# Window attention and shifted blur: queries and keys stacked by way of DRAM, the residual read back in four quarters

## The reference, cut to what matters

```
x = x + L0(_gn(x), w_qkv, w_proj, b_proj, bias_table, rel_index)
x = x + L1(_gn(x), offset)

L0: qkv = einsum('bchw,oc->bohw', x, w_qkv)     # cut into 7x7 windows, 12 heads of 16
    dots = einsum('wnid,wnjd->wnij', q, k) * scale + bias
    out = einsum('wnij,wnjd->wnid', softmax(dots), v)
    return einsum('bchw,oc->bohw', out, w_proj) + b_proj
L1: each of 8 groups of 24 channels is displaced by its own offset, rounded,
    and then filtered with a 5x5 Gaussian that is centred on the offset's rest
```

## Time and profile before

| | before |
|---|---|
| median of 3 runs | 5955.9 us (5952.99 to 5961.64) |
| the profiled execution's own time | 5947.59 us |
| its span in the trace | 5945.8 us |
| PE busy | 5372.8 us, 90% |
| PEld, DVE, ACT, POOL busy | 75%, 72%, 64%, 60% |
| mean granted TensorE clock | 0.936 of full |
| mean rate of the DMA engines | 133 GB/s |

### The profile page before, as it was taken

One profiled execution on the slowest core, in us unless ns is written; L12 is line 12 of the kernel. 1 busy time (PEld: TensorE's weight loads), 2 busy tenths in 40 slices (PEclk: granted clock), 3 DMA queues, 4 the chain that ended last, 5 costly groups with the idle time before them and its releaser, 6 DMA issues.

```text
span 5945.8 us, 259453 instructions
## 1 busy us (share of the span) xinstructions
PE 5372.8 (90%) x98232; PEld 4462.4 (75%) x98232; DVE 4278.6 (72%) x9682; ACT 3798.7 (64%) x8451; POOL 3556.2 (60%) x3940
## 2 busy tenths in 40 slices
PE   4998999999999999999999999999999999999996
PEld 3777777777777777777777777777777777777775
DVE  3777777777777777777777777777777777777773
ACT  1666666666666666667666666666666666666662
POOL 0566556666566666566665566665666655566664
PEclk9999999999999999999999999999999999999996
DMA  2566665666665666655666655666656666656653
GB/s 60 128 139 143 141 139 129 135 138 143 138 138 124 143 136 144 142 133 126 143 137 141 142 132 130 141 139 136 145 125 134 138 141 139 139 128 136 137 129 65
DMA packets 1353356, 790.32 MB, mean 133 GB/s; under 512 B 1187912, under 2 KB 1237512, under 8 KB 1344392
## 3 DMA queue, kind: packets, MB, share of 16 engines
q1 hardware_dynamic: 1352200, 774.03, 58.6%
HBM read 157.09 MB, written 154.14 MB: 52 GB/s over the span
## 4 chain that ended last, share of the span: by engine, by line
PE 37%; SPq 33%; issue 10%; ACT 8%; DVE 6%; DMA 5%; POOL 0%; ACTq 0%; DVEq 0%; POOLq 0%
SPq L414 13%; SPq L420 11%; PE pO L641 6%; SPq L432 5%; PE pT L624 3%; DMA xr<-x_scratch 2%; PE pS L598 2%; PE pS L590 2%; PE pM L509 2%; PE pT L617 2%; PE pT L608 2%; PE pM L511 2%; PE pM L510 1%; PE pO L651 1%; DMA kst<-mix 1%
## 5 line engine op out<-in xcount | busy, mean ns | idle before, releaser
L1222 POOL TENSOR_TENSOR probl<-prob,probh 98x588 f16<-98x588 f32 x1024 | 1332.2, 1301 | 398.3 <-DVE probh L1066 287.8
L1228 POOL TENSOR_TENSOR o<-osb,o 128x192 f16<-128x192 f32 x1024 | 598.6, 585 | 1434.0 <-ACT o L860 1414.9
L641 PEld LDWEIGHTS pO<-vv,probh 98*49 98x49 f16 x24576 | 866.2, 121 | 206.7 <-issue 151.6
L641 PE MATMUL pO<-vv,probh 98*49 98x34 f16 x24576 | 1017.7, 225 | 1.4 <-ACT om L868 1.2
L641 PE MATMUL pO<-vv,probl 98*49 98x34 f16 x12288 | 990.0, 228 | 2.3 <-issue 2.3
L852 ACT ACTIVATE mov<-pT 12x98 f16<-12x98 f32 x1024 | 244.6, 239 | 993.9 <-PE pT L608 992.7
L1051 DVE TENSOR_REDUCE mx<-pS 128x12 f32<-128x588 f32 x1024 | 776.7, 759 | 18.9 <-PE pS L598 6.1
L641 PEld LDWEIGHTS pO<-vv,probl 98*49 98x49 f16 x12288 | 765.9, 121 | 2.4 <-issue 2.4
L847 ACT ACTIVATE prob<-pT 98x588 f32<-98x588 f32 x1024 | 671.7, 656 | 147.0 <-PE pT L624 133.0
L624 PE MATMUL pT<-qst,kst 96*98 96x49 f16 x12288 | 750.8, 207 | 1.0 <-issue 0.8
L590 PE MATMUL pS<-biasT,addb 128*64 128x294 f16 x4096 | 617.5, 310 | 124.9 <-DMA kst<-mix 77.7
(11 more groups left out here) (192 smaller groups left out, 16086.5 us busy)
## 6 DMA issues: line engine op xcount, KB each, us to landing
kst<-kh SPq DMA_DIRECT2D x1536, 98.0 KB, 2.2
qst<-qh SPq DMA_DIRECT2D x1536, 49.0 KB, 2.4
qst<-mix SPq DMA_DIRECT2D x768, 98.0 KB, 2.6
kst<-mix SPq DMA_DIRECT2D x768, 98.0 KB, 2.5
vv<-cv SPq DMA_DIRECT2D x1024, 73.5 KB
xr<-x_scratch SPq DMA_DIRECT2D x64, 1176.0 KB
out<-xr SPq DMA_DIRECT2D x256, 294.0 KB
x_scratch<-xm SPq DMA_DIRECT2D x256, 196.0 KB, 3.2
```

What stands on the lines that cost most here:

```text
L641: mm = pe.matmul(pO[64 * win:64 * win + NT, OW * hp:OW * hp + OW], b[0:98, p % 2, PW * hp + NT * win:PW * hp + NT * win + NT], vv[:, g % 2 ...
L1222: pool.tensor_tensor(probl[0:98, p % 2, :], prob[0:98, p % 2, :], probh[0:98, p % 2, :], ALU.subtract).then_inc(S["pl_p"], 1)
L1228: pool.tensor_tensor(o16[:, p % 2, C:2 * C], osb[:, p % 2, :], o16[:, p % 2, 0:C], ALU.subtract).then_inc(S["ol_p"], 1)
```

## The change

**Stacks.** After g = 1, 3 and 5 SP now writes the whole block (`qh`, `kh` or `mix`, high and low part, 128 partitions) to a new DRAM buffer, `stack_scratch`, in one transfer (`put`). Once it has landed (`put_q`, `put_k`, `put_t`), SP reads the stack out of that buffer: three transfers for blk 0 and three for blk 1, each for 32 partitions and four head pairs, and six for blk 2, each for two head pairs. ACT's waits before it overwrites `qh`, `kh` and `mix` are now for `put_*` and no longer for `stack_*`. In the code `stack` stands one step behind `put`.

**Residual.** `xr` is read in four quarters of the channels, each over all 112 partitions in rows of 5,376 bytes, at steps 6, 10, 12 and 14, each with its own semaphore. POOL waits for quarter n ahead of block 4n. Before the first `store_x1` of image i at step 15, SP waits for all four.

```
+READS = (6, 10, 12, 14)
...
+            def put(i, c, blk):
+
+                name = "qkt"[blk]
+                sp.wait_ge(S["qk_dve"], nth("qk_dve", i, 6 * c + 2 * blk + 2))
+                src = (qh, kh, mix)[blk]
+                sp.dma_start(stacks[c % 2, blk, :, :, 0:src.shape[2]], src[:, :, :]).then_inc(S[f"put_{name}"], 16)
+
             def stack(i, c, blk):
 
-                buf, done = c % 2, S[("stack_q", "stack_k", "stack_t")[blk]]
-
-                sp.wait_ge(S["qk_dve"], nth("qk_dve", i, 6 * c + 2 * blk + 2))
+                buf, name = c % 2, "qkt"[blk]
+                done = S[f"stack_{name}"]
+                sp.wait_ge(S[f"put_{name}"], nth(f"put_{name}", i, 16 * (c + 1)))
+                hps = slice(0, 4) if blk < 2 else slice(4, NHP)
+                n = hps.stop - hps.start
+
+                def rows(part, row, size):
+                    return stacks[buf, blk, row:row + 32 * n, part, 0:size].rearrange("(n p) t -> p n t", n=n)
                 if blk != 1:
-                    src, size = (qh, CHUNK) if blk == 0 else (mix, 2 * CHUNK)
-                    for n, hp in enumerate(range(4) if blk == 0 else range(4, NHP)):
-                        for r, part in enumerate((0, 1, 0)):
-                            at = q_at(hp, 0)
-                            sp.dma_start(qst[32 * r:32 * r + 32, buf, at:at + size],
-                                         src[32 * n:32 * n + 32, part, :]).then_inc(done, 16)
+                    size = CHUNK if blk == 0 else 2 * CHUNK
+                    at = q_at(hps.start, 0)
+                    for r, part in enumerate((0, 1, 0)):
+                        sp.dma_start(qst[32 * r:32 * r + 32, buf, at:at + n * size].rearrange("p (n t) -> p n t", n=n),
+                                     rows(part, 0, size)).then_inc(done, 16)
...
+            def read_x1(i, n):
+
+                cols = slice(CC // 4 * n, CC // 4 * n + CC // 4)
+                sp.dma_start(xr[0:SY, CC // 4 * HW * n:CC // 4 * HW * (n + 1)],
+                             scratch[:, :, cols].rearrange("s y c x -> (s y) (c x)")).then_inc(S[f"xr_in{n}"], 16)
...
+                    qk = before(qk_step, p - 1, prev, att, nxt) if p else None
+                    if qk and qk[2] % 2:
+                        stack(i + qk[0], qk[1], qk[2] // 2)
                     v = before(v_step, p, prev, att, nxt) if p % PPR == 1 else None
                     if v:
                         spread_v(i + v[0], v[1] // 2)
                     qk = before(qk_step, p, prev, att, nxt)
                     if qk and qk[2] % 2:
-                        stack(i + qk[0], qk[1], qk[2] // 2)
+                        put(i + qk[0], qk[1], qk[2] // 2)
+                    if p == 2 * PPC - 1 and prev and att:
+
+                        for n in range(4):
+                            sp.wait_ge(S[f"xr_in{n}"], nth(f"xr_in{n}", i - 1, 16))
...
-                if g == 4 and due("stack_t", i, 192 * c):
-                    act.wait_ge(S["stack_t"], nth("stack_t", i, 192 * c))
+                if g == 4 and due("put_t", i, 16 * c):
+                    act.wait_ge(S["put_t"], nth("put_t", i, 16 * c))
...
                         if b == 0:
-                            pool.wait_ge(S["xr_in"], nth("xr_in", i - 1, 32))
                             pool.wait_ge(S["gn2_dve"], nth("gn2_dve", i - 1, 13))
+                        if b % (NB // 4) == 0:
+                            name = f"xr_in{b // (NB // 4)}"
+                            pool.wait_ge(S[name], nth(name, i - 1, 16))
```

More of the change, by code:

```diff
@@ L136, with build @@
 SET_HOT, SET_GAUSS, SET_EXT, SET_ALL = 7, 25, 35, 50
-def build(nc, x, w_in, b_out, table, rel, offset, cf, ch, scratch, out):
+def build(nc, x, w_in, b_out, table, rel, offset, cf, ch, scratch, stacks, out):
     images = x.shape[0]
@@ L235, in build @@
             "c1_pe", "z_act", "z_dve", "c2_pe", "y_dve")}
-        PER = {"x_in0": 16, "x_in": 48, "x1_out": 256, "xr_in": 32, "y_out": 8 * 16, "stack_q": 192 * NCH,
-               "stack_k": 192 * NCH, "stack_t": 192 * NCH, "gn1_bn": 12, "gn2_bn": 12, "gn1_dve": 8, "gn1_pe": 2, "gn1_pool": 2,
+        PER = {"x_in0": 16, "x_in": 48, "x1_out": 256, "xr_in0": 16, "xr_in1": 16, "xr_in2": 16, "xr_in3": 16, "y_out": 8 * 16, "put_q": 16 * NCH, "put_k": 16 * NCH, "put_t": 16 * NCH, "stack_q": 48 * NCH,
+               "stack_k": 48 * NCH, "stack_t": 96 * NCH, "gn1_bn": 12, "gn2_bn": 12, "gn1_dve": 8, "gn1_pe": 2, "gn1_pool": 2,
                "gn2_dve": 13, "gn2_pe": 3, "gn2_pool": 1, "xnh_a": 16, "xnl_p": 8,
@@ L402, in _ @@
                          .to_broadcast([SY, 2 * POS])).then_inc(S["const_in"], 16)
-            def stack(i, c, blk):
-                buf, done = c % 2, S[("stack_q", "stack_k", "stack_t")[blk]]
-                sp.wait_ge(S["qk_dve"], nth("qk_dve", i, 6 * c + 2 * blk + 2))
-                if blk != 1:
-                    src, size = (qh, CHUNK) if blk == 0 else (mix, 2 * CHUNK)
-                    for n, hp in enumerate(range(4) if blk == 0 else range(4, NHP)):
-                        for r, part in enumerate((0, 1, 0)):
-                            at = q_at(hp, 0)
-                            sp.dma_start(qst[32 * r:32 * r + 32, buf, at:at + size],
-                                         src[32 * n:32 * n + 32, part, :]).then_inc(done, 16)
-                if blk != 0:
[L417 to L421, removed]
+            def put(i, c, blk):
[3 more added lines that the diff above has]
+                sp.dma_start(stacks[c % 2, blk, :, :, 0:src.shape[2]], src[:, :, :]).then_inc(S[f"put_{name}"], 16)
@@ new lines, in stack @@
+            def stack(i, c, blk):
+                buf, name = c % 2, "qkt"[blk]
[5 more added lines that the diff above has]
+                    return stacks[buf, blk, row:row + 32 * n, part, 0:size].rearrange("(n p) t -> p n t", n=n)
+                if blk != 1:
+                    size = CHUNK if blk == 0 else 2 * CHUNK
[3 more added lines that the diff above has]
+                                     rows(part, 0, size)).then_inc(done, 16)
+                if blk != 0:
+                    for r, part in enumerate((0, 0, 1)):
+                        sp.dma_start(kst[32 * r:32 * r + 32, buf, hps, :],
+                                     rows(part, 0 if blk == 1 else 64, 2 * CHUNK)).then_inc(done, 16)
@@ L468, in body @@
                             sp.wait_ge(S["y_out"], nth("y_out", i - 1, 0))
-                        read_x1(0)
-                    if p == 8 and prev:
-                        read_x1(1)
+                        read_x1(i - 1, 0)
+                    if p in READS[1:] and prev:
+                        read_x1(i - 1, READS.index(p))
                     if p in (2, 7) and nxt:
@@ L579, in scores @@
                 if q == 0:
-                    pe.wait_ge(S["stack_q"], nth("stack_q", i, 192 * (c + 1)))
-                    pe.wait_ge(S["stack_k"], nth("stack_k", i, 192 * (c + 1)))
-                    pe.wait_ge(S["stack_t"], nth("stack_t", i, 192 * (c + 1)))
+                    pe.wait_ge(S["stack_q"], nth("stack_q", i, 48 * (c + 1)))
+                    pe.wait_ge(S["stack_k"], nth("stack_k", i, 48 * (c + 1)))
+                    pe.wait_ge(S["stack_t"], nth("stack_t", i, 96 * (c + 1)))
                 if due("max_d", i, p):
@@ L809, in qk_hi @@
                 act.wait_ge(S["qk_pe"], nth("qk_pe", i, 6 * c + g + 1))
[L811 to L814, removed]
-                if g == 4 and due("stack_t", i, 192 * c):
-                    act.wait_ge(S["stack_t"], nth("stack_t", i, 192 * c))
+                if g == 0 and due("put_q", i, 16 * c):
+                    act.wait_ge(S["put_q"], nth("put_q", i, 16 * c))
+                if g == 2 and due("put_k", i, 16 * c):
+                    act.wait_ge(S["put_k"], nth("put_k", i, 16 * c))
+                if g == 4 and due("put_t", i, 16 * c):
+                    act.wait_ge(S["put_t"], nth("put_t", i, 16 * c))
                 blk, t = g // 2, slice(ROW * (g % 2), ROW * (g % 2) + ROW)
@@ L1297 @@
     scratch = nc.dram_tensor("x1_scratch", (2, HW, CC, HW), F32, kind="Internal").ap()
+    stacks = nc.dram_tensor("stack_scratch", (2, 3, 128, 2, 2 * CHUNK), F16, kind="Internal").ap()
     out = nc.dram_tensor("out_0", x.shape, F32, kind="ExternalOutput").ap()
-    build(nc, *aps, scratch, out)
+    build(nc, *aps, scratch, stacks, out)
     r = run(nc, [arrays], core_ids=[0])
```

5 lines of the change are left out of this document (1 added, 4 removed).

## The result

The changed kernel takes 5847.7 us (median of 4 runs) against 5954.4 us of the kernel before in the same comparison: a ratio of 0.9822, with a 95% interval of 0.9801 to 0.9843. That is 1.8% faster. The forecast was 4.4%; the measured time lies nearer to the third case, in which the issue stall stays (5887), than to the forecast (5694). In its mechanism it is neither: the stall at its old place shrank to a third, and part of what that gave came back elsewhere.

What follows compares the result with a forecast made beforehand. Waits and low clock in steps 6 to 15 were taken to bound it. Issue stall -6.3 and residual's wait -2.3 sum to -8.6 us an image, -258 over 30 images: 5694, said as 5690, range 5520 to 5890.

Steps and rivals of the forecast that it cites:

- the third case: Rival: the issue stall ahead of the scores stays, only 2.3 us an image are won, 5887 us; chance 0.24.
- The 14.4 us to give: Steps 6 to 15: average image 64.3 us, image 1 without its waits and clock loss 49.9, so 14.4 can be won.
- The issue stall, -6.3 an image: TensorE's wait for "issue" ahead of the scores goes: 2.9 us of stall and 3.4 of clock an image.
- the stacks' part: Fills by way of DRAM: 21 fewer SP issues a chunk; step 7's wait and clock, 5.8 us an image, priced as unchanged.
- The residual's wait, -2.3 an image: POOL's wait for the residual's read goes with quarters; 2.3 us an image, the rest of the 14.4.
- SP's new wait ahead of the stores: At step 15, SP waits for all residual quarters before the first layer's stores; claimed to cost nothing.
- Chunk 1's round trip: At step 7 the mix block's stacks land 14.7 to 17.5 us after it is ready, against 13.7: late by 1.0 to 3.8.
- SP stops being late: In SP's queue, 21 fewer issues a chunk at 0.68 us free 14 of 45 us.
- The cause that I gave for the stall: At the scores, "issue" was read as a late instruction refill behind residual, input and queries in the DMA rings; an inference.
- a taken branch breaks the prefetch: Skill's rule for instruction fetch: the stall would belong to the loop and stay, giving the third case's time.
- The slower rival: TensorE waits for stacks at steps 15, 23 and 31 too; 4.6 us an image more, 6094 us; chance 0.15.
- The Trainium skill's fixed cost: About 2.0 us a DMA transfer; a `put` would take 3.8 us, chunk 1 in time, giving the second case's time.

Runs made afterwards that it cites:

- Run 7: Changed kernel with the mix block sent directly in 12 transfers (queries and keys out and back) and six idle matmuls on TensorE at step 13: 5577.3 us, ratio 0.9368.
- run 1: Changed kernel's stacks' part alone, with the residual read in halves and POOL's wait as in the kernel before: 6006.9 us, ratio 1.011.
- run 2: Kernel before with only the residual's quarters at steps 6, 10, 12 and 14, stacks filled inside SBUF: 5860.0 us, ratio 0.9867.
- run 3: Changed kernel with six idle matmuls (filler) on TensorE at step 13: 5785.6 us, ratio 0.9731.
- run 8: Kernel before with the residual's quarters and six idle matmuls at step 13, stacks filled inside SBUF: 5850.2 us, ratio 0.9821.
- run 10: Changed kernel with the mix block direct, queries and keys out and back, and the residual in halves as before: 5808.4 us, ratio 0.9724.
- run 9: Kernel before with the residual in quarters at the halves' places, two at step 6 and two at step 8: 5862.6 us, ratio 0.9855.
- run 5: Changed kernel with the mix block sent directly from SBUF to the stacks in 12 transfers, queries and keys out and back: 5665.3 us, ratio 0.9515.

## Why the prediction was wrong

**The 14.4 us to give.** About right, and in the right place. Run 7 takes 12.0 us an image out, all of it in steps 6 to 15 (64.1 to 51.9), though with filler that the change has not. The split of the 14.4 is another matter; the record of the granted clock shows it (us at half clock an image, images 2 to 29, by steps):

```
                               6-8  9-12  13-15
before                         6.8   7.7    6.6
changed                        5.9   1.0    9.6
stacks alone                   5.1   5.2    8.0
quarters alone                 7.4   2.1    7.6
quarters alone, filler 13      7.1   2.3    1.6
changed, filler 13             5.1   1.1    3.3
mix direct                     2.9   0.0    8.3
mix direct, filler 13          2.2   0.1    1.2
```

The prediction knew the first two columns and priced each at 3.4 us. It had no term for the third, because image 1, from which it worked, has no low clock there.

**The issue stall, -6.3 an image.** This is the first step that failed: it took the stall and its clock as gone for good and put what would come in their place at nothing. At the old place the gain was nearly what was forecast. Steps 9 to 12 went from 27.1 to 21.8 us, 5.3 less, and their time at half clock from 7.7 to 1.0 us, which is 3.4 us of full speed. But a third of the stall of step 10 stayed, and new ones came at steps 5 and 6 (19.2 and 16.3 us in all). They belong to the stacks' part, since run 1 has them and run 2 has not, and issue stalls elsewhere are a sign of being wrong that the prediction names; step 5 costs 0.9 us. And in steps 13 to 15 the low clock grew by 3.0 us, and they take 19.0 instead of 18.1. So 3.5 of the 6.3 are left. That this last loss can be had back shows with filler (runs 3, 7 and 8), which takes most of it away whatever the stacks and the residual do. Why it grew when the stall shrank stays open. The kernel before has a hint: its five images with the least low clock in steps 9 to 12 (3.4 us) have 13.0 us of it in steps 13 to 15, the other images of the loop 5.0.

**The residual's wait, -2.3 an image.** The second step that failed. POOL's wait went, 106.1 to 4.7 us, as forecast, and the gain that I tied to it can't be found: steps 12 to 15 went from 23.8 to 23.6. The 2.3 were what was left over after two prices, and no row said that they were POOL's. Image 1's steps 13 to 15 take 16.7 us, the average image's 18.1: so 1.4 of the 2.3 stand where the low clock does and not where POOL waited (steps 11 and 12). Step 12 is 1.0 shorter; its time at half clock went from 1.8 us to nothing, and no run separates that from POOL's wait. SP's new wait ahead of the stores, put at nothing, is 128.4 us in all, 4.1 each; what it costs is not separated either.

**Chunk 1's round trip.** The wait is as forecast: 2.4 us an image, and it is 69.5 / 32 = 2.2. The trip itself was longer than my sum, 18.9 us from the mix `put` to the scores in image 15, with 14.7 to 17.5 forecast. The queue's part of the sum was good to a microsecond: counted from the keys' `put` the mix `put` landed after 16.6 us (17.2 to 20.0 forecast) and the scores came after 25.1 (24.2 to 27.0). What was off is the distance of the two puts, 6.2 instead of 9.5 us, in image 15 as on average, because the keys' `put` went out late, behind `spread_v`. So "SP stops being late" is true for the mix block, for which SP waited 111 times of 128, and not for the keys (3 times). The rings had more room than the sum gave them: their share is 0.72, with 0.75 to 0.82 forecast. In the changed kernel the trip kept the gain from being 9 us an image: the mix block direct takes 5.5 more out, 3.2 of it in steps 6 to 8.

**The cause that I gave for the stall** was half right. The halves cause it (runs 2 and 10), and the fills' form does not (run 1). That it is the load alone is wrong: at the same places the same bytes in quarters leave two thirds of it (run 9). The rule of the Trainium skill ("Runtime: NRT & Kernel Launch", Instruction fetch mechanics) that a taken branch breaks the prefetch is not needed: the stall came and went with the form of transfers inside one and the same loop. That the stall is a refill is still argued and not shown.

**The stacks' part,** priced at no loss and no gain, is worth a loss of 1.1% by itself (run 1) and, in the form in which the last block goes directly, a gain of more than 3% over the quarters alone (run 5 against run 2). One reason would explain both, and the runs agree with it: out and back frees SP of issues, but makes a chain of two landings, and SP stands for the first.

**The slower rival** needed lateness at all four chunks. It happened in run 1 at two of them. In the changed kernel TensorE waited for stacks at step 15 for 8.5 us in all and at step 31 for 3.2, where the forecast had none.

**The Trainium skill's fixed cost** of some 2 us a transfer ("DMA: Bandwidth & Descriptors", Anatomy of one DMA) can't be read off here. The page gives its formula for transfers that GpSimd issues, and these are SP's. A `put` of 0.8 MB had a median of 4.4 us (keys) and 7.8 us (mix) to landing, against its estimate of 3.8 us; none was measured with nothing else in the rings. The mix block's 7.8 is above the 6.4 that the prediction named as a sign of being wrong.

## What to carry to other kernels

A detour by way of DRAM trades issues for latency. Take it for the blocks that have slack, and let the block that is finished last and needed first go directly, even at twelve issues; here that made 1.8% into 4.9%. Before a gain is priced, add up the low clock by steps over all rounds and not over the best one, and don't book what is left over on the nearest wait. A loss that is taken away at one step can come back at the next; filler at such a place was worth 1.6% once the waits were gone. And a queue that paces the kernel takes back what is won elsewhere: if three different edits end at the same time per round, look for it there.

## What the runs showed of the hardware

Form counts beside bytes, as far as one profile of each kernel tells: 1.2 MB twice into 56 partitions in rows of 21,504 bytes goes with 90.4 us of issue stall ahead of the scores, and the same bytes at the same steps over 112 partitions in rows of 5,376 with 59.0. Spread over four steps they go with 30.6, and in the changed kernel with 31.2 at step 10. And a wait for a landing on SP's queue holds up the transfers behind it: in the changed kernel SP stood for 874.3 us for the mix blocks, 6.8 each:

```profile
SPq L426 <- DMA stack_scratch<-mix: 874.3, 128, 11.8
SPq L426 <- DMA stack_scratch<-qh: 554.4, 128, 8.2
SPq L430 <- DMA stack_scratch<-kh: 443.5, 128, 4.8
```
